# adaLN block with causal attention and a routed feed-forward: y kept in its PSUM bank, the split of the row maxima on GpSimd, x loaded and normalised first, new orders on every engine

## What is computed

```python
mod = (silu(c) @ wmod).reshape(8, 6, 1, 128)          # sa, ca, ga, sb, cb, gb
ga = sign(ga) * max(|ga|, 0.25)                       # gb alike
h = layernorm(x) * (1 + ca) + sa
q, k, v = h @ Wq + bq, h @ Wk + bk, h @ Wv + bv       # 16 heads of 8 channels
att = softmax(causal(q k^T / sqrt(8)))
y = (att @ v) @ Wo + bo
x = x + ga * (layernorm(y) * gamma + beta)
h = layernorm(x) * (1 + cb) + sb
x = x + gb * (sum over the top 2 of 8 experts of coef * (silu(h Wg) * (h Wu)) Wd + shared expert)
```

## Time and profile before

| | |
|---|---|
| median of 3 runs | 592.57 us (589.27 to 598.64) |
| the profiled execution's own time | 592.91 us |
| its span, first to last instruction | 591.2 us |
| TensorE (PE) busy | 520.3 us, 88% |
| VectorE (DVE) busy | 416.9 us, 71% |
| ScalarE (ACT) busy | 299.3 us, 51% |
| GpSimd (POOL) busy | 244.5 us, 41% |
| mean granted TensorE clock | 0.916 |

### The profile page before, as it was taken

How to read it: one execution, slowest core, us unless ns; L and a number is a source line. 1 busy time by engine, 2 the same in 40 slices (tenths; PEclk the granted TensorE clock), 3 DMA queues, 4 the chain that set the end, 5 groups by cost and what they waited for, 6 DMA issues and landing times.

```text
span 591.2 us, 10213 instructions
## 1 busy us (share of the span) xinstructions
PE 520.3 (88%) x3628; PEld 281.4 (48%) x3643; DVE 416.9 (71%) x877; ACT 299.3 (51%) x614; POOL 244.5 (41%) x299
## 2 busy tenths in 40 slices
PE   1647989899989999899989998999989998999567
PEld 1513434455644464456455554546445643645234
DVE  7458988687776868776878777686767677573045
ACT  1104546656565546655565647454655646455320
POOL 6024335713662257524572366235742424034210
PEclk9957899899997999899989999899979998599769
DMA  5171412321324113321332132412331121001000
GB/s 139 48 191 51 148 46 83 107 74 42 77 59 149 42 51 87 112 54 45 84 103 81 42 78 59 149 42 60 77 131 24 37 82 38 0 2 37 0 1 18
DMA packets 46930, 40.65 MB, mean 69 GB/s; under 512 B 8088, under 2 KB 42656, under 8 KB 46880
## 3 DMA queue, kind: packets, MB, share of 16 engines
q1 hardware_dynamic: 39232, 36.92, 22.1%
q10 hardware_dynamic: 7648, 3.09, 2.0%
HBM read 24.91 MB, written 14.68 MB: 67 GB/s over the span
## 4 chain that ended last, share of the span: by engine, by line
PE 72%; DVE 13%; ACT 6%; issue 4%; DMA 2%; SPq 1%; POOL 0%; DVEq 0%; POOLq 0%; ACTq 0%
PE pv_bank L1044 13%; PE s_bank L1015 11%; PE s_bank L1030 10%; DVE row_max L844 7%; PE gate_bank L1097 6%; PE gate_bank L1130 6%; PE up_bank L1108 6%; PE misc L973 5%; PE s_bank L1017 4%; PE misc L995 3%; ACT probs L650 3%; PE misc L1000 2%; PE up_bank L1068 2%; PE misc L1078 2%; ACT square L676 2%
## 5 line engine op out<-in xcount | busy, mean ns | idle before, releaser
L844 DVE TENSOR_REDUCE row_max<-s_bank 128x1 f32<-128x512 f32 (+3 forms) x352 | 213.0, 637 | 82.1 <-PE s_bank L1017 79.5
L650 ACT ACTIVATE probs<-s_bank 128x512 f32<-128x512 f32 x320 | 183.4, 598 | 105.9 <-PE s_bank L1030 103.4
L1015 PE MATMUL s_bank<-k_stack,q_stack 72*128 72x256 bf16 (+3 forms) x512 | 142.4, 319 | 17.2 <-DMA k_stack<-k_scr 8.3
L558 POOL TENSOR_SCALAR_AFFINE_SELECT probs<-probs 128x512 f32<-128x512 f32 (+1 forms) x96 | 80.2, 841 | 120.5 <-ACT probs L650 120.4
L1030 PE MATMUL s_bank<-q_stack,k_stack 75*128 75x128 bf16 (+3 forms) x512 | 118.7, 310 | 3.8 <-ACT probs L650 1.7
L1017 PE MATMUL s_bank<-causal,ident_bf 128*128 128x128 bf16 x512 | 103.8, 228 | 0.0
L1044 PE MATMUL pv_bank<-probs,v_aug 128*32 128x512 f32 (+3 forms) x1024 | 97.3, 485 | 0.0
L1015 PEld LDWEIGHTS s_bank<-k_stack,q_stack 72*128 72x128 bf16 x512 | 51.0, 100 | 81.1 <-DVE row_max L844 49.7
L1030 PEld LDWEIGHTS s_bank<-q_stack,k_stack 75*128 75x128 bf16 x512 | 42.0, 100 | 48.2 <-ACT probs L650 17.5
L1017 PEld LDWEIGHTS s_bank<-causal,ident_bf 128*128 128x128 bf16 x512 | 52.3, 102 | 24.3 <-issue 16.6
L543 POOL TENSOR_TENSOR hidden<-hidden,coef_sb 128x512 f32<-128x512 f32 x28 | 35.6, 1271 | 43.2 <-ACT coef_sb L696 43.0
(11 more groups left out here) (150 smaller groups left out, 625.2 us busy)
## 6 DMA issues: line engine op xcount, KB each, us to landing
q_stack<-q_scr SPq DMA_DIRECT2D x96, 96.0 KB
k_stack<-k_scr SPq DMA_DIRECT2D x96, 96.0 KB
k_scr<-k_parts SPq DMA_DIRECT2D x14, 256.0 KB, 3.2
q_scr<-q_parts SPq DMA_DIRECT2D x7, 384.0 KB, 2.3
k_scr<-k_parts SPq DMA_DIRECT2D x7, 384.0 KB, 3.0
x_res<-in_L_attn_x SPq DMA_DIRECT2D x8, 256.0 KB, 3.4
out_x<-out_sb SPq DMA_DIRECT2D x8, 256.0 KB, 2.6
x_in<-in_L_attn_x ACTq DMA_DIRECT2D x7, 256.0 KB, 2.9
```

Source lines behind the costliest of these rows:

```text
L558: nc.gpsimd.affine_select(out=view, in_=view, compare_op=ALU.is_ge, fill=0.0, base=0, pattern=pat, channel_multiplier=-1).then_inc(probs_r ...
L650: nc.scalar.activation(dst, src, ACT.Exp, scale=SCALE).then_inc(exp_done, 1)
L844: nc.vector.reduce_max(row_max[s % 2][:, 0, h:h + nh, qt], s1_bank[u % 2][:, 0:nh * w].rearrange("p (h k) -> p h k", h=nh), AX_X).then_inc ...
L1015: nc.tensor.matmul(dst[:, w * i:w * (i + 1)], q_stack[0:KROWS, h, P * qt:P * (qt + 1)], k_stack[0:KROWS, h, 0:w], start=True, stop=False)
```

## The change

It does four things.

1. y stays in `up_bank`: yn scales it there in place, yg multiplies it there, x2 reads it there. The tile `y_sb` is gone, and yn no longer waits for the last batch's x2. The first up product (u0) now waits for x2 in place of yn, since it takes the same bank.
2. The two subtractions of msplit are issued by GpSimd in place of VectorE, with the same waits.
3. In the prologue the load of x comes first on SyncE's queue. The copy `cond_rep` is a task of its own, `spread`, between q and k, and the four `gates` stand behind v.
4. All the tables of steps are new, on all engines.

```diff
-PV_STEPS = [[23, 0, 2, 4], [26, 2, 8, 8], [27, 0, 3, 3], [29, 0, 1, 1]]
+PV_STEPS = [[24, 0, 0, 0], [25, 4, 8, 8], [28, 0, 0, 4], [29, 0, 10, 14]]
...
 PROLOGUE = [(0, *numbered(name)) for name in (
-    "xin", "xs", "cond", "xn", "late", "xt", "gates0", "q", "gates1", "k", "gates2", "stack", "v", "gates3")]
+    "xin", "xs", "cond", "xn", "late", "xt", "q", "spread", "k", "stack", "v", "gates0", "gates1", "gates2", "gates3")]
...
+            sp.dma_start(x_in[:, :, :], tok(x, 0)).then_inc(x_in_ready, 16)
             sp.dma_start(cond_sb[:, :], cond).then_inc(cond_in, 16)
             sp.dma_start(wmod_sb[:, :], wmod).then_inc(cond_in, 16)
-            sp.dma_start(x_in[:, :, :], tok(x, 0)).then_inc(x_in_ready, 16)
...
+                if name == "msplit":
+
+                    z = row_max[s % 2][:, :, :, :].rearrange("p k h t -> p k (h t)")
+                    n2 = it * (G * 2) + 2 * s
+                    pool.wait_ge(s1_reduced, it * (G * U1) + U1 * (s + 1))
+                    nc.gpsimd.tensor_tensor(z[:, 1, :], z[:, 0, :], upper(z[:, 0, :]), ALU.subtract).then_inc(max_step, 1)
+                    pool.wait_ge(max_step, n2 + 1)
+                    nc.gpsimd.tensor_tensor(z[:, 2, :], z[:, 1, :], upper(z[:, 1, :]), ALU.subtract).then_inc(max_step, 1)
...
-            act.wait_ge(ct_step, 6)
+            act.wait_ge(ct_step, 5)
...
                 if name == "yn":
-                    need(act, x2_ready, it - 1)
                     act.wait_ge(y_rstd, it)
                     for t in range(TT):
-                        final = nc.scalar.activation(y_sb[:, t, :], up_bank[:, P * t:P * (t + 1)], ACT.Copy,
-                                                     scale=rstd["y"][:, t:t + 1])
+                        y = up_bank[:, P * t:P * (t + 1)]
+                        final = nc.scalar.activation(y, y, ACT.Copy, scale=rstd["y"][:, t:t + 1])
...
+            def spread():
+
                 dve.wait_ge(ct_step, 5)
                 nc.vector.tensor_copy(cond_rep[:, :, :], cond_T[:, :].unsqueeze(2).to_broadcast([P, B, P])).then_inc(ct_step, 1)
...
                 if name == "yg":
                     dve.wait_ge(y_scaled, it)
-                    nc.vector.tensor_tensor(y_sb[:, :, :], y_sb[:, :, :], over_tiles(gamma_a[:, it - 1, :]),
-                                            ALU.mult).then_inc(y_gamma, 1)
+                    y = up_bank[:, :].rearrange("p (t c) -> p t c", t=TT)
+                    nc.vector.tensor_tensor(y, y, over_tiles(gamma_a[:, it - 1, :]), ALU.mult).then_inc(y_gamma, 1)
...
-                    nc.vector.tensor_tensor(x2[:, :, :], y_sb[:, :, :], x_res[:, :, :], ALU.add).then_inc(x2_ready, 1)
+                    nc.vector.tensor_tensor(x2[:, :, :], up_bank[:, :].rearrange("p (t c) -> p t c", t=TT), x_res[:, :, :], ALU.add).then_inc(x2_ready, 1)
...
                     if a == 0:
-                        pe.wait_ge(y_scaled, it)
+                        pe.wait_ge(x2_ready, it)
```

More of the change, by code:

```diff
@@ L94 @@
-LAST = ["y", "ystat", "yn", "yg", "x2", "x2stat", "x2n", "x2t", "lg", "route", "prob", "above", "rank", "g0", "g1",
-        "u0", "ct", "g2", "u1", "g3", "u2", "c0", "g4", "u3", "u4", "c1", "down0", "c2", "down1", "down2", "c3",
+    0: {0: [("xin", "next"), ("wdb", "prev"), ("uev", ""), ("xs", "next")], 5: [("o", "")], 14: [("xn", "next")],
+        15: [("msplit", "cur")], 19: [("xres", "prev")], 23: [("mod0", "first"), ("xt", "next")],
+        25: [("max", "cur")], 27: [("mod1", "first")]},
@@ new lines @@
+    3: {1: [("u1", "prev"), ("g2", "prev")], 10: [("u2", "prev")], 11: [("msplit", "cur"), ("ct", "prev")],
+        14: [("g3", "prev"), ("c0", "prev")], 15: [("uev", "")], 16: [("u3", "prev")], 17: [("c1", "prev")],
+        19: [("g4", "prev")], 27: [("c2", "prev")], 28: [("u4", "prev")],
+        29: [("down0", "prev"), ("c3", "prev"), ("down1", "prev"), ("max", "cur"), ("down2", "prev"), ("down3", "prev"), ("down4", "prev"), ("fin", "prev"), ("o", "")]},
+}
+LAST = ["y", "ystat", "yn", "yg", "x2", "x2stat", "x2n", "x2t", "lg", "route", "prob", "above", "g0", "u0", "rank",
+        "g1", "g2", "u1", "ct", "g3", "u2", "u3", "c0", "g4", "c1", "u4", "c2", "down0", "down1", "down2", "c3",
@@ L298, in block_kernel @@
         oT = sb("oT", [P, T])
-        x_res, y_sb, x2, x2_n = (sb(x, [P, TT, C]) for x in ("x_res", "y_sb", "x2", "x2_n"))
+        x_res, x2, x2_n = (sb(x, [P, TT, C]) for x in ("x_res", "x2", "x2_n"))
         h2T = sb("h2T", [P, T])
@@ L823, in run @@
                     condition()
+                if name == "spread":
+                    spread()
                 if name == "gates":
```

36 lines of the change are left out of this document (11 added, 25 removed), and 31 rows, old and new, of tables (LATER, S1_STEPS, S2_STEPS).

## The result

| | before | after |
|---|---|---|
| median, 4 runs of each | 593.93 us | 563.6 us |
| lowest and highest | 589.27 to 598.64 | 562.6 to 565.53 |
| ratio after / before | | 0.9518, 95% interval 0.9448 to 0.9588 |
| the profiled execution's own time, and its span | 592.91, 591.2 | 562.72, 561.0 |
| mean granted clock of TensorE | 0.916 | 0.957 |

The kernel is faster by 4.8%. The forecast was 566 us in a range of 552 to 586. Some executions of a kernel are over 1.5% longer than its fastest one; the ratios and their intervals leave them out and the medians do not, so that a ratio can differ from the quotient of two medians by up to 1%.

A forecast was written before the change was run, and what follows sets the result against it. TensorE's row, gaps and slow clock were taken to bound steady batches, VectorE batch 0. Prologue 4.4, batch 0 2.6, splits 9.1 and clock 10.5 sum to 26.6 us off 592.9: 566.3, predicted 566, range 552 to 586.

The forecast's parts named there:

- the collision: Section 1: VectorE's second msplit subtraction takes 1.18 us beside GpSimd's x_res, not 0.18; TensorE stands 1.43 us.
- Splits on GpSimd: Steady batches: msplit on GpSimd saves 1.3 us a batch, times seven, -9.1 us.
- The walk: Section 1, times from y's end T: split ends T + 3.3, transpose about T + 3.8, v starts T + 5.05.
- The clock: Batches 1 to 6 and the last: slow clock worth 21.0 us, half taken as gained, -10.5 (0 to -21).
- the first rival: Slow clock hangs on the 1.43 us gap alone: all 21.0 us go in place of 10.5, 556 us; chance 0.20.
- y in its bank: yg, multiplying in PSUM, goes to 0.69 us; nothing in the sum, but +6 us if it stays at 1.57.
- Prologue: Program start: cond_rep (4.13 us) and first gate product (1.71) leave the path, 1.4 comes back: -4.4 us.
- Batch 0: VectorE bounds batch 0 and sheds four splits; three fifths of 4.35 us taken: -2.6 us (-1 to -4).
- Tail: Behind the last pv: yg already takes 0.69 us and LAST only moves pieces: 0 (-1 to +1).

The follow-up runs named there:

- b_xres: Kernel before with one table number changed, so GpSimd does x_res ahead of the deviation of y in section 1: 565.13 us, ratio 0.9616.
- b_y: Kernel before with only y kept in its bank (yn, yg and x2 in place, u0 behind x2): 590.57 us, ratio 1.0001.
- b_gapfill: Kernel before with six unused matmuls on TensorE ahead of section 1's transpose of the maxima, filling the gap: 570.03 us, ratio 0.961.
- a_split_dve: Kernel after with the split back on VectorE, right behind the last maximum of each section: 570.33 us, ratio 0.9638.
- a_ysb: Kernel after with y written to SBUF again (y_sb), all else as after: 575.43 us, ratio 0.971.
- a_fill: Kernel after with GpSimd's fill of v_aug held back until x_n is done: 563.67 us, ratio 0.9531.
- best_1: Kernel after with old LAST, x_res ahead of the deviation of y, v_aug fill behind x_n, down-weight loads behind h1T: 562.24 us, ratio 0.9474.
- a_xres: Kernel after with one number changed, so GpSimd does x_res ahead of the split in section 1: 569.94 us, ratio 0.9701.
- b_split: Kernel before with msplit alone moved to GpSimd, in the old tables: 585.33 us, ratio 0.9915.
- a_last: Kernel after with the list LAST of the kernel before: 562.84 us, ratio 0.9515.
- b_split_y: Kernel before with the split on GpSimd and y in its bank, all tables else as before: 579.31 us, ratio 0.9784.

## Why the prediction was right in its sum, and where it was off

The sum, 566.3 us, came within 4 us of the profiled execution's 562.7, and part of that is luck: the prologue and batch 0 gave 5.0 us less than forecast, the slow clock in batches 1 to 6 gave 8.1 more, and these errors cancel in part.

- **What bounds the kernel, and the collision:** right, and shown. The gap of 1.43 us came of the second subtraction beside x_res. b_xres parts the two with one number and wins 20.3 us in batches 1 to 6 alone (386.1 to 365.8). It frees yg as well, but yg freed alone brings nothing (b_y).
- **Splits on GpSimd, -9.1 at 1.3 a batch.** The size held for what it covers: 22.5 us less 15.1 for the clock (b_gapfill) leaves 7.4 in six batches, 1.2 a batch. The walk held as well: split end forecast at T + 3.3 and found at T + 3.1, transpose T + 3.8 and T + 3.5, v T + 5.05 and T + 4.6, with the stall for ScalarE where it was put. The reason given was half right, though: a_split_dve shows that by the new order alone the collision goes, and the engine matters for 0.4 us.
- **The clock, "I take half": -10.5.** This is the term that failed in size. All of the 34 us in batches 1 to 6 went, 15.1 us in place of 7.0. The price of 1.4 us for a stretch of 3.4 was right (15.1 / 34 x 3.4 = 1.5). What failed was the reason for halving it, that TensorE's row from y to v is "about the same work" in nearly the same time: b_gapfill keeps that order and that lateness and only fills the gap, and the slow clock is gone. This was the first rival, with 0.20; its 556 us were not reached because the start did not give its part. In the last batch and tail 27.4 us of slow clock are left of 38.4, worth 11.0 / 3.4 x 1.4 = 4.5 of the 5.7 us won there: the stretch of 17.1 us is gone, and what stands behind it has grown by 6.
- **y in its bank, 0 in the sum and +6 "if it stays at 1.57".** Both held in their way. yg takes 0.70 in all eight batches. Alone it brings nothing (b_y, 1.0001); taken out of the new order it costs 1.2 us a batch (a_ysb), 7.0 us over batches 1 to 6. The Trainium skill has the rule, in "SBUF — State Buffer", section "Who interferes with whom", that a VectorE instruction with at most one SBUF input, outside the modes that use both port pairs, isn't held by GpSimd. The rows of yg, x2 and fin agree: 0.70 beside x_res with the bank, 1.19 with two SBUF tiles. The prediction told the rule without that exception, and x_n, which has one SBUF input and was held, would fall under it.
- **Prologue, -4.4: wrong, 0.6.** The step that failed is "cond_rep takes 4.13 us ahead of x_n. ... Both leave this path". Its own work is 0.69 us, as it shows at its new place at 20.81 us. The other 3.4 came of GpSimd's fill of v_aug, which in the new order holds x_n in place of cond_rep (a_fill). The prediction saw the fill ("its present length falls in GpSimd's filling of constants") but not that x_n would take its place in it. And it left out ScalarE's DMA issues, next in line behind it (a_fill); with both out of the way the first score product comes 3.4 us sooner (best_1). The gates, moved behind v, no longer keep TensorE busy between q, k and v; k and v now take 2.08 us each, where they took 1.12 and 1.16.
- **Batch 0, -2.6: 1.4 measured, which proves nothing.** With the same instructions it takes from 51.9 to 58.7 us, the longer ones with more slow clock (a_xres). How much the splits are worth there stays open. That they could cost something was not foreseen: on the old tables the gap before two transposes grew to 2.44 us (b_split), and in the kernel after the one of section 0 is 1.37 us, where it was 0.96.
- **Tail, 0:** from the end of the last y to the end of the program 36.0 us in place of 34.4, so +1.6, beyond the stated 1. The old list in the new kernel takes 35.2 (a_last), but so does the unchanged tail in b_gapfill; the list is at most part of it. There are 4.4 us more of slow clock in this stretch (18.9 in place of 14.5).

How the parts stand to each other: from the kernel before, batches 1 to 6 go from 386.1 us to 371.0 when the gap is filled, to 365.8 when x_res moves out of the collision, and to 363.6 with all of the change. GpSimd's split alone moves x_res onto yg and opens a gap in section 3 (0.9915); the bank for y repairs the first (0.9784), the new tables the second (0.9518).

**What stays open.** The clock's fall is not told by the length of a gap alone. In section 1, 1.42 or 1.43 us of standing brought it in every batch that was looked at, 0.87 in one of six, 0.63 in every second one (b_split_y) or in one of six (b_split), 0.41 never (b_xres). Elsewhere gaps of 1.33 in section 3 (b_split) and of 1.16 to 1.44 in section 2 (a_ysb) didn't bring it. What sets section 1 apart, whether the work ahead of it or the place in time, was not tried by itself.

## What to carry to other kernels

Before an instruction is moved to another engine, look whether one number in the order parts the two that collide: here that alone brought four fifths of the gain or more. A gap of 1.4 us on TensorE in a steady loop can cost more by the slow clock behind it (2.5 us a batch here) than by itself; fill the gap with matmuls that do nothing, and one run prices the clock apart from the lateness. When an instruction takes several times as long as its likes, look at what runs beside it, and ask what that will stretch next once this one is moved away: here the fill of v_aug went from cond_rep to x_n, and x_res from the subtraction to yg. And before a difference in one stretch is put down to an edit, compare that stretch in kernels where the edit does not touch it: batch 0 varied by 6.8 us in this way.
